# Block-diagonal keys of the second and third layer written by ScalarE instead of by copies through DMA

## The chip, the cores and the metric

One core of a Trainium2 chip runs the whole program. The metric is device time in microseconds (us); lower is better. The engines are TensorE (PE; PEld is its weight load), VectorE (DVE), ScalarE (ACT), GpSimd (POOL) and SyncE (SP, which here only issues transfers). SPq is SP's queue of transfers.

## The reference

Four transformer blocks run one after another on x of 32 x 128 x 256, with a context of the same shape. The change touches the second and the third block, which have the same form:

```
Q, K, V = split into 16 heads of 16 (x @ wq + bq, kv @ wk + bk, kv @ wv + bv)
A       = softmax(Q K^T / 4, masked)
x       = layernorm(x + (A V) @ wo + bo)          # self attention: kv = x
x       = the same once more with kv = context     # cross attention
x       = layernorm(x + relu(x @ w1 + b1) @ w2 + b2)
```

All is computed in float32. A product is made of three fp32r products of a high and a low part (L97).

## The kernel before

`phase16_full` computes the second layer and then, as a program section of its own, the third. The first layer is two sections before them, and the fourth layer (`Track`, tags "fourth") comes behind. A round is two of the 32 batch rows, 256 tokens, so a layer has 16 rounds (`ROUNDS2`). Tensors of the second layer have names with `second_`, those of the third `third_`.

The order on each engine is written out by hand in one `body(r)` per engine, and the engines meet through semaphores (`wait_ge`). One body has four steps, here called x0, x1, y0 and y1. In each step TensorE first makes the scores of the attention half that comes next (`pe_scores`, mask matmuls L1576 and score matmuls L1584), then turns the probabilities of the present half (`pe_turn`, L1595, four per step) and mixes those with V (`pe_mix`, L1608 and L1614). Between these it does projections, feed-forward products and the transposes of the norms (`Norm16.pe`, L1729) of other rounds, up to four rounds apart. ScalarE takes the exponentials (`act_exp`, L1641; four groups of four per step, t = 0 to 3), VectorE the maxima (L1621) and the copies of the turned probabilities (L1627).

The keys are made in step x1 for the self attention of the next round and in step y1 for the cross attention of this one. TensorE's `pe_k` leaves them in the shared PSUM bank `EV_BANK`; the next user of the bank waits until it is read. ScalarE's `act_k` (L1377) adds the bias and writes `a_k`. It stands between the exponentials t = 0 and t = 1 of the step. Behind t = 1 come `act_spread` (L1532) and the norm's `act` and `act_hi` (L1738 and L1746).

Two neighbouring heads have their scores made by one matmul with 32 rows, so a key operand `k_block` is needed with a second copy of the 256 tokens, in which the rows of the other head are zero. `pool_setup` sets `k_block` to zero once, and SP then copies the 16 rows of each head to their place (`sp_k`, L1402: 8 heads in each of 2 column groups, 16 copies of 16 x 256). `k_block` lies in `stage`, the buffer through which the weights come in at a layer's start. `pe_scores` waits for the copies. SP issues the copies in the same queue as the loads of the next inputs.

What of this runs at a layer's start, before the first body, is written at the end of each engine's function: the weights' split, K, Q and V of round 0, and the first scores.

## Time and profile before

| | us |
|---|---|
| median of 3 runs | 3672.21 (3661.26 to 3674.09) |
| the profiled execution, its own time | 3672.43 |
| its span in the trace | 3670.7 |
| TensorE busy | 3180.7 (87%) |
| VectorE busy | 2038.8 (56%) |
| ScalarE busy | 1938.2 (53%) |
| GpSimd busy | 1642.5 (45%) |

The busy times are sums over the whole program. The second layer lies at about 1520 to 2415 us of the span, the third at about 2415 to 3300 us.

### The profile page before, as it was taken

The numbers are of one execution on the slowest core, as the hardware profiler recorded it, in microseconds if no ns is written. First come the engines' busy times: TensorE is split into PE (matmuls) and PEld (weight loads), VectorE is DVE, ScalarE is ACT, GpSimd is POOL, SyncE is SP. The second block draws the span as 40 slices with busy tenths as digits, with TensorE's granted clock in tenths as the row PEclk, the third lists the DMA queues.
The fourth block names the chain that finished last, engine by engine and source line by source line (L and its number), as shares of the span: only waits on it lengthen the run. The fifth ranks groups of instructions, "written<-read, shape, count | busy, mean of one in ns | idle before, by whom it ended". The sixth has DMA issues, their size and how long they took to land. (4 is left out here: it accounts for less than half of the span.)

```text
span 3670.7 us, 79460 instructions
## 1 busy us (share of the span) xinstructions
PE 3180.7 (87%) x27248; PEld 2716.9 (74%) x27248; DVE 2038.8 (56%) x4126; ACT 1938.2 (53%) x7862; POOL 1642.5 (45%) x2020
## 2 busy tenths in 40 slices
PE   8999996899999998379999999737999999956987
PEld 5998895688888887357888888626888888754664
DVE  3455553444444444346777777525677777734665
ACT  2444442333333333156777777425777777635775
POOL 1223222024444435324666666622566666662444
PEclk9999998999999999779999999957999999988999
DMA  3112112101111110311221221021111111113231
GB/s 114 50 46 66 60 37 105 60 27 35 49 49 49 49 46 18 119 40 46 60 62 58 62 62 53 25 103 38 42 55 57 57 57 57 42 33 106 85 98 55
DMA packets 192554, 213.61 MB, mean 58 GB/s; under 512 B 30209, under 2 KB 161537, under 8 KB 189697
## 3 DMA queue, kind: packets, MB, share of 16 engines
q1 hardware_dynamic: 192384, 211.40, 18.1%
q8 instruction: 101, 1.65, 0.2%
q14 instruction: 69, 0.56, 0.1%
HBM read 131.59 MB, written 58.72 MB: 52 GB/s over the span
## 5 line engine op out<-in xcount | busy, mean ns | idle before, releaser
L1641 ACT ACTIVATE second_stage<-second_psum,second_neg_max 128x128 f32<-128x128 f32 x1024 | 362.7, 386 | 206.7 <-DVE second_neg_max L1621 206.4
L1641 ACT ACTIVATE third_stage<-third_psum,third_neg_max 128x128 f32<-128x128 f32 x1024 | 362.6, 386 | 193.4 <-DVE third_neg_max L1621 193.1
L1641 ACT ACTIVATION_READ_ACCUMULATOR second_stage<-second_psum,second_neg_max 128x1 f32 x1024 | 231.5, 226 | 0.0
L1641 ACT ACTIVATION_READ_ACCUMULATOR third_stage<-third_psum,third_neg_max 128x1 f32 x1024 | 231.1, 226 | 0.0
L534 POOL TENSOR_TENSOR cross_ff_hidden_lo<-cross_ff_relu,cross_ff_hidden_hi 128x256 fp32r<-128x256 f32 x128 | 93.3, 730 | 288.5 <-DVE cross_ff_hidden_hi L529 288.5
L1621 DVE TENSOR_REDUCE second_neg_max<-second_psum 128x4 f32<-128x512 f32 x256 | 169.2, 684 | 53.8 <-PE second_psum L1584 51.4
L1621 DVE TENSOR_REDUCE third_neg_max<-third_psum 128x4 f32<-128x512 f32 x256 | 168.7, 682 | 41.1 <-PE third_psum L1584 40.1
L1524 ACT ACTIVATE fourth_stage<-fourth_psum,fourth_neg_max 128x128 f32<-128x128 f32 x512 | 181.7, 386 | 3.8 <-DVE fourth_neg_max L1500 3.8
L1595 PE MATMUL third_psum<-third_eye,third_stage 128*128 128x128 f32 x1024 | 165.0, 285 | 16.8 <-DVE third_p_turned_odd L1627 7.9
L1595 PE MATMUL second_psum<-second_eye,second_stage 128*128 128x128 f32 x1024 | 162.8, 283 | 14.4 <-DVE second_p_turned_odd L1627 7.4
L529 DVE CAST cross_ff_hidden_hi<-cross_ff_relu 128x256 fp32r<-128x256 f32 x128 | 45.4, 355 | 209.7 <-ACT cross_ff_relu L524 209.6
L1595 PEld LDWEIGHTS third_psum<-third_eye,third_stage 128*128 128x128 f32 x1024 | 118.5, 144 | 46.4 <-issue 25.1
L1595 PEld LDWEIGHTS second_psum<-second_eye,second_stage 128*128 128x128 f32 x1024 | 118.2, 143 | 40.8 <-issue 21.2
L415 ACT ACTIVATE cross_arena<-cross_psum,cross_neg_max 128x128 f32<-128x128 f32 x256 | 90.4, 365 | 95.6 <-DVE cross_neg_max L448 95.6
L415 ACT ACTIVATE self_arena<-self_psum,self_neg_max 128x128 f32<-128x128 f32 x256 | 90.5, 366 | 84.6 <-DVE self_neg_max L448 84.6
L464 DVE TENSOR_TENSOR self_attended_lo<-self_psum,self_attended_hi 128x512 fp32r<-128x512 f32 x64 | 44.3, 692 | 159.4 <-ACT self_attended_hi L428 159.4
L1545 POOL COPY third_inverse_row<-third_inverse 128x128 f32<-128x128 f32 x128 | 33.9, 294 | 211.7 <-DVE third_inverse L1512 176.3
L524 ACT ACTIVATE cross_ff_relu<-cross_psum,cross_cols 128x256 f32<-128x256 f32 x128 | 60.7, 474 | 124.5 <-PE cross_psum L97 122.7
L1707 POOL TENSOR_SCALAR second_n_z<-second_n_z,second_n_moments,second_n_rstd 128x256 f32<-128x256 f32 x96 | 117.1, 1225 | 10.3 <-POOL second_n_rstd L1702 10.3
L1707 POOL TENSOR_SCALAR third_n_z<-third_n_z,third_n_moments,third_n_rstd 128x256 f32<-128x256 f32 x96 | 117.0, 1225 | 10.2 <-POOL third_n_rstd L1702 10.2
L1545 POOL COPY second_inverse_row<-second_inverse 128x128 f32<-128x128 f32 x128 | 34.0, 294 | 189.7 <-DVE second_inverse L1512 189.7
L1506 DVE COPY fourth_stage<-fourth_psum 128x512 f32<-128x512 f32 x128 | 87.7, 685 | 51.1 <-PE fourth_psum L1459 51.1
(438 smaller groups left out, 12548.7 us busy)
## 6 DMA issues: line engine op xcount, KB each, us to landing
second_stage<-second_a_k SPq DMA_DIRECT2D x512, 16.0 KB, 1.8
third_stage<-third_a_k SPq DMA_DIRECT2D x512, 16.0 KB, 1.8
cross_arena<-in_l0b_packed SPq DMA_DIRECT2D x6, 1024.0 KB, 4.9
self_arena<-in_l0a_packed SPq DMA_DIRECT2D x4, 1024.0 KB, 6.2
self_x_raw<-in_x_t SPq DMA_DIRECT2D x8, 512.0 KB, 3.8
self_x_rows<-in_x_rows SPq DMA_DIRECT2D x8, 512.0 KB, 3.9
self_ct_raw<-in_ctx_t SPq DMA_DIRECT2D x8, 512.0 KB, 4.3
context_hi<-self_ct_hi SPq DMA_DIRECT2D x8, 512.0 KB, 5.0
```

The source lines that it names most:

```text
L415: ins = act.activation(sh.p[:, h % 2, b, :], psum[:, S8_BANK, b * SEQ:(b + 1) * SEQ], ACT.Exp, bias=sh.neg_max[:, h % 2, b:b + 1], accum_o ...
L464: dve.tensor_tensor(self.sh.attended.lo[:, h % 2, :], psum[:, MIX8_BANK, :], f32(self.sh.attended.hi[:, h % 2, :]), ALU.subtract) \
L524: act.activation(self.relu[:, t % HIDDEN_SLOTS, :], psum[:, bank, 0:HALF], ACT.Relu, bias=self.b1[:, t % M:t % M + 1]).then_inc(self.hidde ...
L529: dve.tensor_copy(self.hidden.hi[:, t % HIDDEN_SLOTS, :], self.relu[:, t % HIDDEN_SLOTS, :]) \
L534: pool.tensor_tensor(self.hidden.lo[:, t % HIDDEN_SLOTS, :], self.relu[:, t % HIDDEN_SLOTS, :], f32(self.hidden.hi[:, t % HIDDEN_SLOTS, :] ...
L1506: dve.tensor_copy(self.sh.p_turned[:, h % 4, :, :], psum[:, TURN_BANK, :].rearrange("p (x k) -> p x k", x=4)) \
L1524: ins = act.activation(self.sh.p[:, h % 4, x, :], psum[:, SCORE_BANKS[h % 4], x * SEQ:(x + 1) * SEQ], ACT.Exp, bias=self.sh.neg_max[:, h % ...
L1545: ins = pool.tensor_copy(self.sh.inverse_row[:, b, k * P:(k + 1) * P].rearrange("p (g d) -> p g d", g=8), self.sh.inverse[:, b, k * 8:(k + ...
L1595: ins = pe.transpose(banks.psum[:, TURN_BANK, x * SEQ:(x + 1) * SEQ], self.sh.p_wide[:, 4 * b + t, x, :], self.sh.eye[:])
L1621: dve.tensor_reduce(self.sh.neg_max[:, 4 * b + t, :], psum[:, SCORE_BANKS[t], :].rearrange("p (x k) -> p x k", x=4), AX_X, ALU.max, negate ...
L1641: ins = act.activation(self.sh.p_wide[:, 4 * b + t, x, :], psum[:, SCORE_BANKS[t], x * SEQ:(x + 1) * SEQ], ACT.Exp, bias=self.sh.neg_max[: ...
L1707: pool.tensor_scalar(self.z[:, b, :], self.z[:, b, :], self.moments[:, b, 0:1], self.rstd[:, b:b + 1], ALU.subtract, ALU.mult) \
```

## The change

ScalarE writes both halves of `k_block` itself. `act_k` is four activations instead of two: for each column group c and each parity e it writes 256 columns, with a scale that is one [128,1] column of `parity` (1 in the rows of the heads with that parity, 0 in the others) and a bias that is multiplied with the same column, so that the other heads' rows come out as zero. The buffer `a_k`, the 16 copies per call and the zeroing by GpSimd are gone. `act_k` now waits for the scores of the round before, and `pe_scores` for `k_ready` instead of the copies. VectorE makes `parity` and the biases once per layer at its start. The fourth layer keeps the copies.

```diff
@@ -1316,11 +1316,11 @@
 class Project16:
 
 
-    def __init__(self, kit, name, w):
+    def __init__(self, kit, name, w, keys=True):
         sb = kit.sb
         self.w = w
         self.q = sb(name + "_q", [P, C, T2], F32)
-        self.k = sb(name + "_k", [P, C, T2], F32)
+        self.k = sb(name + "_k", [P, C, T2], F32) if keys else None
         self.v = sb(name + "_v", [P, B2, C, 4, 2, 32], F32)
         self.v_slots = [self.v[:, b].rearrange("p c j e f -> p (c j) (e f)").rearrange(
             "p g (x d) -> p g x d", d=DK)[:, :, 0:4:3, :] for b in range(B2)]
@@ -1329,7 +1329,8 @@
         self.q_ready = kit.counter(name + "_q_ready", 1)
         self.k_in_psum = kit.counter(name + "_k_in_psum", 1)
         self.k_ready = kit.counter(name + "_k_ready", C)
-        self.k_blocked = [kit.counter(f"{name}_k_blocked{c}", 16 * 8) for c in range(C)]
+        if keys:
+            self.k_blocked = [kit.counter(f"{name}_k_blocked{c}", 16 * 8) for c in range(C)]
         self.v_in_psum = kit.counter(name + "_v_in_psum", 1)
         self.v_ready = kit.counter(name + "_v_ready", 1)
 
@@ -1555,6 +1556,26 @@
                            ALU.subtract).then_inc(self.lo_ready.sem, 1)
 
 
+class ProjectWide(Project16):
+
+
+
+    def __init__(self, kit, name, w, k_block, sh):
+        Project16.__init__(self, kit, name, w, keys=False)
+        self.k_block, self.sh = k_block, sh
+
+    def act_k(self, act, r, psum, scores_read):
+
+        act.wait_ge(scores_read.sem, scores_read.at(r, 0))
+        act.wait_ge(self.k_in_psum.sem, self.k_in_psum.at(r, 1))
+        for c in range(C):
+            for e in range(2):
+                ins = act.activation(self.k_block[:, c, e, :], psum[:, EV_BANK, c * T2:(c + 1) * T2],
+                                     ACT.Identity, bias=self.w["k_bias_of"][:, e, c:c + 1],
+                                     scale=self.sh.parity[:, e:e + 1])
+            ins.then_inc(self.k_ready.sem, 1)
+
+
 class AttendWide(Attend16):
 
 
@@ -1564,8 +1585,7 @@
     def pe_scores(self, pe, r, banks, b):
         if b == 0:
             pe.wait_ge(self.proj.q_ready.sem, self.proj.q_ready.at(r, 1))
-            for c in range(C):
-                pe.wait_ge(self.proj.k_blocked[c].sem, self.proj.k_blocked[c].at(r, 16 * 8))
+            pe.wait_ge(self.proj.k_ready.sem, self.proj.k_ready.at(r, C))
             if self.mask is not None:
                 pe.wait_ge(self.mask.ready.sem, self.mask.ready.at(r, 1))
         tokens = slice(b * SEQ, (b + 1) * SEQ)
@@ -1873,6 +1893,9 @@
         self.spread = sb("spread", [P, B2, DM], F32)
         self.mix = sb("mix", [P, B2, DM], F32)
         self.attended = Split(kit, "attended", [P, C, T2])
+        if wide:
+            self.in_head = sb("in_head", [P, 8], F32)
+            self.parity = sb("parity", [P, 2], F32)
         self.minus_half = sb("minus_half", [P, 4], F32)
         self.eye = sb("eye", [P, P], F32)
 
@@ -1904,6 +1927,8 @@
             self.ct = Split(kit, "ct", [P, C, T2])
             self.x_rows = kit.sb("x_rows", [P, B2, DM], F32)
             self.residual = kit.sb("residual", [P, B2, DM], F32)
+            self.k_bias_of = [kit.sb(f"k_bias{i}", [P, 2, C], F32) for i in range(2)]
+            self.parity_made = kit.counter("parity_made", 0)
         self.small_loaded = kit.counter("small_loaded", 0)
         self.hi_made = kit.counter("w_hi_made", 0)
         self.lo_made = kit.counter("w_lo_made", 0)
@@ -1943,7 +1968,7 @@
         n = str(i + 1)
         return {"q": self.take(i * 2048, 512, DM), "k": self.take(i * 2048 + 512, 512, DM),
                 "v": self.take(i * 2048 + 1024, 512, DM), "q_bias": self.colv("q" + n),
-                "k_bias": self.colv("k" + n), "v_row": self.rowv("v" + n)}
+                "k_bias": self.colv("k" + n), "k_bias_of": self.k_bias_of[i] if self.extra else None, "v_row": self.rowv("v" + n)}
 
     def out_of(self, i):
         return self.take(i * 2048 + 1536, 512, DM)
@@ -1993,7 +2018,7 @@
                 if not m.per_batch:
                     m.pool(pool, 0)
         pool.wait_ge(consts.sem, made)
-        for s in range(2):
+        for s in range(0 if self.extra else 2):
             pool.wait_ge(self.lo_made.sem, min(s + 1, self.slots))
             pool.memset(sh.stage[:, s * sh.block_cols:(s + 1) * sh.block_cols], 0.0) \
                 .then_inc(self.block_zeroed.sem, 1)
@@ -2026,8 +2051,7 @@
         kit, sh, psum, mask = layer.kit, layer.sh, layer.psum, layer.mask
         xt, ct, rowv, colv = layer.xt, layer.ct, layer.rowv, layer.colv
         stored = kit.counter("stored", 32)
-        proj1, proj2 = (Project16(kit, f"a{i + 1}", layer.weights_of(i)) for i in range(2))
-        proj1.k_block, proj2.k_block = sh.k_block
+        proj1, proj2 = (ProjectWide(kit, f"a{i + 1}", layer.weights_of(i), sh.k_block[i], sh) for i in range(2))
         att1, att2 = (AttendWide(kit, f"a{i + 1}", (proj1, proj2)[i], mask[i], layer.out_of(i), sh)
                       for i in range(2))
         y1_rows = kit.sb("y1_rows", [P, B2, DM], F32)
@@ -2106,16 +2130,12 @@
                     store(Back(r, 4), r, 4)
                 if ok(0) and not (isinstance(r, int) and r == 0):
                     load_context(r, r, 0)
-                if ok(1):
-                    proj1.sp_k(sp, Back(r, -1))
                 if ok(2):
                     load_mask(mask[0], Back(r, -2), r, -2)
                 if ok(1):
                     load_rows(Back(r, -1), r, -1)
                 if ok(2):
                     load_x(Back(r, -2), r, -2)
-                if ok(0):
-                    proj2.sp_k(sp, r)
                 if ok(1):
                     load_mask(mask[1], Back(r, -1), r, -1)
 
@@ -2126,8 +2146,6 @@
             load_mask(mask[0], 0, 0, 0)
             load_mask(mask[1], 0, 0, 0)
             load_x(1, 1, 0)
-            sp.wait_ge(layer.block_zeroed.sem, 2)
-            proj1.sp_k(sp, 0)
             load_mask(mask[0], 1, 1, 0)
             for r in range(FULL_FIRST):
                 body(r)
@@ -2171,7 +2189,7 @@
 
                 exp(x1_next, 0)
                 if ok(1):
-                    proj1.act_k(act, Back(r, -1), psum)
+                    proj1.act_k(act, Back(r, -1), psum, att1.scores_ready)
                 exp(x1_next, 1)
                 spread(x1)
                 if ok(-2):
@@ -2194,7 +2212,7 @@
 
                 exp(y1_next, 0)
                 if ok(0):
-                    proj2.act_k(act, r, psum)
+                    proj2.act_k(act, r, psum, att2.scores_ready)
                 exp(y1_next, 1)
                 spread(y1)
                 if ok(0):
@@ -2206,7 +2224,8 @@
                 exp(y1_next, 3)
 
             act.wait_ge(layer.lo_made.sem, layer.slots)
-            proj1.act_k(act, 0, psum)
+            act.wait_ge(layer.parity_made.sem, 3)
+            proj1.act_k(act, 0, psum, att1.scores_ready)
             proj1.act_q(act, 0, psum)
             for t in range(4):
                 att1.act_exp(act, 0, psum, 0, t)
@@ -2223,11 +2242,23 @@
             for proj in (proj1, proj2):
                 dve.memset(proj.v[:], 0.0).then_inc(layer.zeroed.sem, 1)
             layer.dve_split_weights(dve, 0)
+            dve.wait_ge(layer.consts.sem, 2)
+            dve.tensor_reduce(sh.in_head[:], sh.eye[:].rearrange("p (h d) -> p h d", d=DK), AX_X, ALU.max) \
+               .then_inc(layer.parity_made.sem, 1)
+            dve.wait_ge(layer.parity_made.sem, 1)
+            dve.tensor_reduce(sh.parity[:], sh.in_head[:].rearrange("p (a e) -> p e a", e=2), AX_X, ALU.max) \
+               .then_inc(layer.parity_made.sem, 1)
+            dve.wait_ge(layer.parity_made.sem, 2)
             dve.wait_ge(layer.small_loaded.sem, 16 * 3)
             for i in range(2):
                 dve.tensor_scalar(colv(f"q{i + 1}"), colv(f"q{i + 1}"), DK ** -0.5, None, ALU.mult)
             dve.tensor_tensor(rowv("s1"), rowv("s1"), rowv("o2"), ALU.add)
             dve.tensor_tensor(rowv("s2"), rowv("s2"), rowv("ff"), ALU.add)
+            for i in range(2):
+                for e in range(2):
+                    ins = dve.tensor_scalar(layer.k_bias_of[i][:, e, :], colv(f"k{i + 1}"),
+                                            sh.parity[:, e:e + 1], None, ALU.mult)
+            ins.then_inc(layer.parity_made.sem, 1)
             for norm in (norm1, norm2, norm3):
                 ins = dve.memset(norm.stats[:], 0.0)
             ins.then_inc(layer.biases.sem, 1)
```

Three places in the order of the instructions. First, SP's queue at the start of the second layer; before:

```order
L2079 DMA second_ct_lo<-context_lo 128x2x256
L2085 DMA second_x_rows<-x_rows 128x2x256
L1836 DMA second_mask_ints<-in_mask_self 128x2x128
L1836 DMA second_mask_ints<-in_mask_cross 128x2x128
L2072 DMA second_xt_hi<-x_hi 128x2x256
L2072 DMA second_xt_lo<-x_lo 128x2x256
L1402 DMA second_stage<-second_a_k 16x256 x16
L1836 DMA second_mask_ints<-in_mask_self 128x2x128
L1402 DMA second_stage<-second_a_k 16x256 x16
L1836 DMA second_mask_ints<-in_mask_self 128x2x128
L2085 DMA second_x_rows<-x_rows 128x2x256
```

The same place in the changed kernel:

```order
L2103 DMA second_ct_lo<-context_lo 128x2x256
L2109 DMA second_x_rows<-x_rows 128x2x256
L1856 DMA second_mask_ints<-in_mask_self 128x2x128
L1856 DMA second_mask_ints<-in_mask_cross 128x2x128
L2096 DMA second_xt_hi<-x_hi 128x2x256
L2096 DMA second_xt_lo<-x_lo 128x2x256
L1856 DMA second_mask_ints<-in_mask_self 128x2x128 x2
L2109 DMA second_x_rows<-x_rows 128x2x256
```

The sixteen copies of round 0, and those of every later round, are gone; the loads behind them move up and keep their order.

Second, ScalarE in step x1 of the loop of the second layer, from the exponentials t = 0 to t = 2; before:

```order
L1641 ACTIVATE second_stage,second_sums<-second_psum,second_neg_max 128x128 x4
L1374 REGISTER_ALU
L1375 REGISTER_ALU
L1377 ACTIVATE second_a_k<-second_psum,second_cols 128x256 x2
L1638 REGISTER_ALU
L1641 ACTIVATE second_stage,second_sums<-second_psum,second_neg_max 128x128 x4
L1532 COPY second_spread<-second_psum 128x256
L1738 ACTIVATE second_n_y<-second_psum,second_cols 128x256 x2
L1746 CAST second_n_yt_hi<-second_n_y 128x512
L1638 REGISTER_ALU
L1641 ACTIVATE second_stage,second_sums<-second_psum,second_neg_max 128x128 x4
```

The same place in the changed kernel:

```order
L1661 ACTIVATE second_stage,second_sums<-second_psum,second_neg_max 128x128 x4
L1569 REGISTER_ALU
L1570 REGISTER_ALU
L1573 ACTIVATE second_stage<-second_psum,second_k_bias,second_parity 128x256 x4
L1658 REGISTER_ALU
L1661 ACTIVATE second_stage,second_sums<-second_psum,second_neg_max 128x128 x4
L1533 COPY second_spread<-second_psum 128x256
L1758 ACTIVATE second_n_y<-second_psum,second_cols 128x256 x2
L1766 CAST second_n_yt_hi<-second_n_y 128x512
L1658 REGISTER_ALU
L1661 ACTIVATE second_stage,second_sums<-second_psum,second_neg_max 128x128 x4
```

The two activations that wrote `a_k` are four that write `k_block` in `stage`, ahead of the same instructions.

Third, VectorE at the start of the second layer in the changed kernel:

```order
L2002 TENSOR_TENSOR second_w_lo<-second_stage,second_w_hi 128x2048
L2246 TENSOR_REDUCE second_in_head<-second_eye 128x8
L2249 TENSOR_REDUCE second_parity<-second_in_head 128x2
L2254 TENSOR_SCALAR second_cols<-second_cols 128x2 x2
L2255 TENSOR_TENSOR second_rows<-second_rows,second_rows_extra 128x256
L2256 TENSOR_TENSOR second_rows<-second_rows,second_rows_extra 128x256
L2259 TENSOR_SCALAR second_k_bias<-second_cols,second_parity 128x2 x4
L2263 MEMSET second_n_stats 128x12 x3
L2002 TENSOR_TENSOR second_w_lo<-second_stage,second_w_hi 128x2048 x3
```

L2246, L2249 and L2259 are new, six small instructions between the splits of the first and of the second part of the weights.

## Rows read from the trace of the kernel before

**Rows 1.** The page's slices: busy tenths of TensorE and its clock, 40 slices.

```profile
PE   8999996899999998379999999737999999956987
PEclk9999998999999999779999999957999999988999
```

**Rows 2.** Windows: busy us of PE, PEld, DVE, ACT, POOL; clock, DMA share, GB/s.

```profile
1560.00:1580.00 20.00, 11.40 (x52) 5.45 (x52) 6.60 (x11) 9.42 (x53) 0.53 (x2) 0.50 0.04 10
1900.00:2000.00 100.00, 97.43 (x1029) 83.14 (x1019) 72.56 (x155) 73.20 (x331) 66.45 (x87) 1.00 0.21 62
2900.00:3000.00 100.00, 95.64 (x1026) 82.27 (x1026) 73.39 (x160) 73.27 (x333) 63.27 (x84) 1.00 0.21 63
```

**Rows 3.** TensorE's waits, second layer: us in total, times, longest us.

```profile
PE second_psum L1576 <- DMA second_stage<-second_a_k: 12.9, 1, 12.9
PE second_psum L97 <- DVE second_n_yt_lo L1752: 7.4, 13, 1.3
PEld second_psum L97 <- ACT second_n_y L1738: 3.7, 15, 1.3
```

**Rows 4.** Timeline, starts of both layers: start, us, what, [idle before <- releaser].

```profile
1541.48 2.17 POOL L1849 TENSOR_SCALAR second_mask_flags<-second_mask_ints 128x256 bf16<-128x256 int32 x1 [2.48 <-issue]
1543.00 0.84 ACT L1377 ACTIVATE second_a_k<-second_psum,second_cols 128x256 f32<-128x256 f32 x2 [2.41 <-DVE second_w_lo L1977]
1550.79 10.08 SPq L1402 DMA_DIRECT2D second_stage<-second_a_k  x16
1562.31 1.87 PE L1576 MATMUL second_psum<-second_mask_flags,second_mask_eye 128*128 128x512 bf16 x4 [12.87 <-DMA second_stage<-second_a_k]
2462.77 1.87 PE L1576 MATMUL third_psum<-third_mask_flags,third_mask_eye 128*128 128x512 bf16 x4 [12.84 <-DMA third_stage<-third_a_k]
```

**Rows 5.** Two ScalarE lines: duration ns min/median/max.

```profile
L1377 ACT ACTIVATE second_a_k<-second_psum,second_cols x64: 466/488/498, 1543.0 to 2316.1; 128x256 f32<-128x256 f32 x64
L1738 ACT ACTIVATE second_n_y<-second_psum,second_cols x96: 553/564/625, 1605.8 to 2411.2; 128x256 f32<-128x256 f32 x96
```

**Rows 6.** Timeline, second layer, one step x1.

```profile
1959.76 0.85 ACT L1377 ACTIVATE second_a_k<-second_psum,second_cols 128x256 f32<-128x256 f32 x2
1960.47 0.39 ACT L1641 ACTIVATE second_stage<-second_psum,second_neg_max 128x128 f32<-128x128 f32 x1
1961.58 0.63 PE L1729 MATMUL second_psum<-second_eye,second_n_z 128*128 128x128 f32 x4 [0.16 <-POOL second_n_z L1707]
1961.84 0.43 ACT L1532 COPY second_spread<-second_psum 128x256 f32<-128x256 f32 x1
1962.32 1.02 ACT L1738 ACTIVATE second_n_y<-second_psum,second_cols 128x256 f32<-128x256 f32 x2
1963.37 0.63 ACT L1746 CAST second_n_yt_hi<-second_n_y 128x512 fp32r<-128x512 f32 x1
1964.03 1.63 DVE L1752 TENSOR_TENSOR second_n_yt_lo<-second_n_y,second_n_yt_hi 128x512 fp32r<-128x512 f32 x1 [0.38 <-ACT second_n_yt_hi L1746]
1965.71 0.38 PE L97 MATMUL second_psum<-second_n_yt_hi,second_w_lo 128*128 128x256 f32 x1 [0.51 <-DVE second_n_yt_lo L1752]
```

**Rows 7.** Timeline, second layer, one step y1.

```profile
1934.62 0.37 ACT L1641 ACTIVATE second_stage<-second_psum,second_neg_max 128x128 f32<-128x128 f32 x1 [4.27 <-DVE second_neg_max L1621]
1936.00 0.85 ACT L1377 ACTIVATE second_a_k<-second_psum,second_cols 128x256 f32<-128x256 f32 x2
1938.52 1.02 ACT L1738 ACTIVATE second_n_y<-second_psum,second_cols 128x256 f32<-128x256 f32 x2
1939.59 0.19 PEld L97 LDWEIGHTS second_psum<-second_n_yt_hi,second_w_lo 128*128 128x128 f32 x1 [0.17 <-ACT second_n_y L1738]
```

**Rows 8.** Timeline, third layer, one step x1.

```profile
3000.47 1.02 ACT L1738 ACTIVATE third_n_y<-third_psum,third_cols 128x256 f32<-128x256 f32 x2 [0.27 <-PE third_psum L1729]
3003.66 0.39 PE L97 MATMUL third_psum<-third_n_yt_hi,third_w_lo 128*128 128x256 f32 x1 [0.32 <-DVE third_n_yt_lo L1752]
```

**Rows 9.** Timeline, second layer, step x1 of round 1.

```profile
1629.86 0.66 PE L1595 MATMUL second_psum<-second_eye,second_stage 128*128 128x128 f32 x4 [1.85 <-DVE second_p_turned_odd L1627]
```

## The prediction

> **What bounds the kernel now.** I read the slices of the page first, then windows of the two layers, the waits, and last the timeline of single steps. TensorE is the busy engine nearly everywhere [rows 1], and in the middle of the second and the third layer it is busy 96 to 97 us in 100 at full clock, while ScalarE is at 73 [rows 2]. So in the steady part only what makes TensorE wait costs time, and almost nothing does. The copies of the keys appear in its waits exactly once in the second layer, with 12.9 us [rows 3]: that is the layer's start. In every later round the copies are issued and landed a step or two before the scores that need them. They are 16 instructions in 10.08 us of SP's queue [rows 4], and hidden.
>
> What TensorE does wait for in the steady part is short and comes often: 13 times the low part of a norm's output (7.4 us in all), which VectorE makes in step x1, and 15 times ScalarE's L1738 ahead of a weight load (3.7 us), in step y1 [rows 3]. Both come from one chain on ScalarE: exponentials, keys, exponentials t = 1, spread, norm, cast. The keys stand in the middle of it, in both steps. This matters more than ScalarE's busy share.
>
> **The start of a layer: a gain.** Before, ScalarE writes round 0's keys at 1543.00 [rows 4], TensorE does Q and V, and then stands 12.87 us until the sixteen copies have landed; in the third layer 12.84 us [rows 4]. After the change nothing is copied. The first scores then need Q and K, which are both read before V is computed, and the mask flags, which GpSimd has finished at 1541.48 + 2.17 = 1543.65 [rows 4]. So they can follow V at once. The longer `act_k` gives back a part, since Q's product waits for the bank that it reads. Its new length comes from rows 5 and 6. An activation with one column operand (the bias) takes 488 ns, and a pair takes 0.85 us, the next instruction starting 0.71 us after the pair's start, or 0.355 us for each. L1738 has the same shape with two column operands, bias and scale, as the new ones have: 564 ns [rows 5], and a pair takes 1.02 us [rows 6], so the second starts 1.02 - 0.56 = 0.46 us behind the first. Four of these hold the engine for 4 x 0.456 = 1.82 us and end after 3 x 0.456 + 0.564 = 1.93 us. The bank is free 1.93 - 0.85 = 1.08 us later. Gain: 12.87 - 1.08 = 11.8 us and 12.84 - 1.08 = 11.8 us, together 23.5.
>
> The Trainium skill (ScalarE: Activation LUTs, What ACT_TABLE_LOAD costs) puts 93 ns on each column operand and says that activations back to back overlap by 93 ns; the rows have 76 ns for the operand and about 0.11 to 0.13 us for the overlap. By the page's figures, 280 ns + 0.833 ns per column with one operand, four activations instead of two would add 4 x 0.49 - 2 x 0.40 = 1.17 us where the rows give 1.11; over the calls below that is an estimate of 66 us instead of 63. I take the rows.
>
> VectorE's six new small instructions lie between the first split of the weights and the second, where ScalarE and VectorE wait for the weights' transfers. I cost them at nothing. Without that cover they are about 1 us a layer, by my estimate. GpSimd's zeroing went beside other work and gives nothing.
>
> A second part of the start is the clock. After the long wait the first 20 us of the fill ran at a granted 0.50, the lower level, with TensorE busy 11.40 us [rows 2]. If the wait is gone, a part of that work may run at the upper level. Between nothing and half of the busy time (5.7 us) lies the gain; much of the fill is ScalarE's and VectorE's chain, so I take 2 us a layer, 4 in all.
>
> **Every later call: a loss.** ScalarE goes on after `act_k` 1.82 - 0.71 = 1.11 us later. What stands behind it?
>
> Step x1, second layer [rows 6]. The exponentials t = 1 start at 1960.47 as soon as the keys are issued, spread at 1961.84, L1738 at 1962.32, the cast at 1963.37, VectorE's low part at 1964.03, and TensorE's L97 at 1965.71, having waited 0.51 us. ScalarE has no gap in this chain, and TensorE waits at its end already. So the whole 1.11 us arrives at TensorE. A second way leads there too: the transposes L1729 need the bank that the keys free. The keys ended at 1960.61 and now end at 1961.69, and TensorE started L1729 at 1961.58. That is hardly 0.2 us, and it lies inside the 1.11.
>
> Step y1, second layer [rows 7]. The keys are at 1936.00, L1738 ends at 1939.54, and TensorE's weight load for the next feed-forward product starts at 1939.59, having waited 0.17 us for just that. Again there is no slack: another 1.11 us.
>
> Then ScalarE stands idle 4.27 us at the start of the next key step, until the maxima come [rows 7], which follow TensorE's scores. The delay is therefore not carried on; ScalarE, VectorE and TensorE are all later by the same amount, and the next step has its old relations. For the same reason nothing gives the time back: TensorE's other short waits are for chains that moved with it.
>
> Third layer, x1 [rows 8]: L1738 had waited 0.27 us for TensorE's transposes, so 1.11 - 0.27 = 0.84 us pass on; TensorE's L97 waited 0.32 us at the end. Its y1 I take like the second layer's.
>
> Calls: 32 a layer, one of them at the start, 15 in x1 and 16 in y1. In x1 the call of round 0 falls into the fill with idle ScalarE, and I cost it at nothing. Round 1 has no norm there, but the turned probabilities hang on spread, for which TensorE waited 1.85 us [rows 9], so it pays in full. That leaves 14 + 16 = 30. Second layer: 30 x 1.11 = 33.3. Third: 13 x 0.84 + 17 x 1.11 = 29.8. Together 63.1 us.
>
> The scores' own wait for the copies and SP's earlier loads are worth nothing in the steady part; no load appears among the waits that I list [rows 3].
>
> **The sum.** 63.1 - 23.5 - 4 = +35.6 us. The profiled execution took 3672.4, as the median of the runs did (3672.2), so 3672.4 + 35.6 = 3708.0.
>
> **The rivals.**
> Half absorbed: only one of the two key steps passes its delay on. For it speaks that the waits at the chain's end are short (0.17 and 0.32 us), so that an unseen reserve of queued TensorE work might cover them; against it, that there is a wait at all. 31.5 - 27.5 = +4: 3676.
> Faster: the two chains take the longer `act_k` without TensorE feeling it, for instance because the four activations overlap more tightly than L1738's, and only the start counts: -27.5, 3645. The point from which the change is a gain is 23.5 / 60 = 0.39 us per call, where the rows say 1.11 for the engine; even a scale column that costs nothing leaves two more at 0.355 us, 0.71 us per call. So this needs slack that no row shows.
> No start gain: something else holds the first scores or the fill swallows the 23.5 us, and the full loss stays: +63, 3735. The mask flags are ready, but TensorE's first products in the fill hang on chains that may have other ends.
> That the change doesn't do what it says I exclude: the copies are gone from the queue.
>
> **How the numbers follow.** Full loss with start gain 0.66 (by itself 3692 to 3722, which takes the clock at its two ends and some tenths per call), half absorbed 0.15, faster 0.07, no start gain 0.12. A measurement of this kernel tells about 0.5%, 18 us, from no change. Slower: 0.66 + 0.12, less 0.02 for the lower edge, 0.76. Same: 0.15 + 0.02, 0.17. Faster 0.07. The range 3678 to 3730 leaves out the faster case (0.07), half of the half absorbed one (0.07) and a part of the last (0.05).
>
> **What would show it.** In the profile after: no DMA at the first scores, and the scores of each layer about 11.8 us earlier against the layer's start. Four key activations near 564 ns each, 1.8 us from the first to the next exponential. In x1 TensorE's wait for the low part near 1.6 us instead of 0.5 (1.2 in the third layer), in y1 a wait of about 1.2 us for L1738; a round 2.2 us longer in the second layer, 1.95 in the third. The prediction is wrong if the rounds keep their length, if the start doesn't shrink, or if the clock falls in the steady part.

## The result, and the profile after

The changed kernel takes 3706.8 us, the median of 4 runs (3703.7 to 3709.9); the kernel before, on the same chip, 3669.6 (3661.3 to 3674.1). The ratio is 1.010, with a 95% interval of 1.008 to 1.013: the change costs about 1%. The profiled execution took 3704.3 us, with a span of 3702.6, which is 31.9 more than the span before.

The page of the changed kernel: totals of the engines, and TensorE's row and clock row in the 40 slices.

```profile
PE 3176.7 (86%) x27123; PEld 2715.3 (73%) x27248; DVE 2049.2 (55%) x4138; ACT 2007.1 (54%) x7990; POOL 1641.2 (44%) x2016
...
PE   8999996889999997479999999747999999866887
...
PEclk9999998999999998689999999968999999988998
```

The slices can hardly be told from those of before [rows 1]; a loss of 1 us in every 24 doesn't show there. The windows do show it (columns as in [rows 2]: length, busy us of PE, PEld, DVE, ACT, POOL, clock, DMA share, GB/s).

```profile
1560.00:1580.00 20.00, 15.46 (x133) 12.05 (x126) 8.80 (x15) 8.96 (x39) 3.31 (x5) 0.64 0.06 18
1900.00:2000.00 100.00, 93.82 (x972) 79.15 (x965) 69.69 (x149) 73.54 (x322) 62.80 (x83) 1.00 0.15 47
2900.00:3000.00 100.00, 92.55 (x966) 79.58 (x966) 69.45 (x149) 75.70 (x333) 59.65 (x78) 1.00 0.13 42
```

In the middle of the two layers TensorE is busy 93 to 94 us in 100 where it was 96 to 97, at the same full clock. ScalarE's share is hardly higher, though each round gives it about 2.2 us more to do, because the round has become as much longer. The clock stays at its upper level in these stretches, so it has no part in the loss. In the first row, the fill, TensorE does more in the same 20 us than before, and the granted clock is 0.64 instead of 0.50; but the fill now begins 14 us earlier (rows below), so the row is a later part of it. Over the same stage, from the first scores to the key activations of y1 in round 0, the granted clock is 0.72 instead of 0.69, and in the third layer 0.77 instead of 0.68.

The starts of both layers, timeline (start, us, what, [idle before <- releaser]):

```profile
1538.37 2.05 POOL L1869 TENSOR_SCALAR second_mask_flags<-second_mask_ints 128x256 bf16<-128x256 int32 x1 [20.41 <-DMA second_mask_ints<-in_mask_self]
1539.78 1.93 ACT L1573 ACTIVATE second_stage<-second_psum,second_k_bias,second_parity 128x256 f32<-128x256 f32 x4 [2.41 <-DVE second_w_lo L2002]
...
1548.36 1.93 PE L1596 MATMUL second_psum<-second_mask_flags,second_mask_eye 128*128 128x512 bf16 x4
...
2467.97 1.31 PE L1596 MATMUL third_psum<-third_mask_flags,third_mask_eye 128*128 128x512 bf16 x4
```

The scores start 1548.36 - 1539.78 = 8.58 us behind the first key activation, where it was 1562.31 - 1543.00 = 19.31 [rows 4]: a gain of 10.7 us. The third layer has 8.58 as well, and gains 11.9. The four activations take 1.93 us, and TensorE has no wait for a DMA left.

One step x1 in the middle of the second layer, timeline, the step that answers to [rows 6]:

```profile
1961.58 1.95 ACT L1573 ACTIVATE second_stage<-second_psum,second_k_bias,second_parity 128x256 f32<-128x256 f32 x4
1963.38 0.41 ACT L1661 ACTIVATE second_stage<-second_psum,second_neg_max 128x128 f32<-128x128 f32 x1
1963.58 0.66 PE L1749 MATMUL second_psum<-second_eye,second_n_z 128*128 128x128 f32 x4 [0.34 <-ACT second_stage L1573]
...
1965.00 1.11 ACT L1758 ACTIVATE second_n_y<-second_psum,second_cols 128x256 f32<-128x256 f32 x2
...
1966.63 0.66 PE L1615 MATMUL second_psum<-second_eye,second_stage 128*128 128x128 f32 x4 [0.53 <-DVE second_p_turned_odd L1647]
1966.80 1.78 DVE L1772 TENSOR_TENSOR second_n_yt_lo<-second_n_y,second_n_yt_hi 128x512 fp32r<-128x512 f32 x1 [0.22 <-ACT second_n_yt_hi L1766]
1968.63 0.39 PE L97 MATMUL second_psum<-second_n_yt_hi,second_w_lo 128*128 128x256 f32 x1 [0.63 <-DVE second_n_yt_lo L1772]
```

From the first key activation to the next exponential it is 1963.38 - 1961.58 = 1.80 us, as forecast; before, 0.71 [rows 6]. TensorE now waits three times in this step, 0.34 us for the keys themselves at L1749, 0.53 us for the turned probabilities, and 0.63 us for the low part. Before, it waited 0.16 us at the same transposes, for GpSimd's `n_z`, and 0.51 us for the low part.

The step y1 that answers to [rows 7]:

```profile
1986.88 1.95 ACT L1573 ACTIVATE second_stage<-second_psum,second_k_bias,second_parity 128x256 f32<-128x256 f32 x4
1988.88 0.66 PE L1749 MATMUL second_psum<-second_eye,second_n_z 128*128 128x128 f32 x4 [0.35 <-ACT second_stage L1573]
...
1991.47 0.39 PE L97 MATMUL second_psum<-second_n_yt_hi,second_w_lo 128*128 128x256 f32 x1 [0.78 <-ACT second_n_y L1758]
```

TensorE's waits over the whole second layer, 1520 to 2420 us (us in total, times, longest):

```profile
PE second_psum L1615 <- DVE second_p_turned_odd L1647: 16.8, 18, 3.0
PE second_psum L97 <- ACT second_n_y L1758: 13.3, 16, 1.1
PE second_psum L1749 <- POOL second_n_z L1727: 12.4, 5, 6.0
PE second_psum L1749 <- ACT second_stage L1573: 11.8, 27, 2.6
...
PE second_psum L97 <- DVE second_n_yt_lo L1772: 8.9, 13, 1.3
```

The same view before:

```profile
PE second_psum L1729 <- POOL second_n_z L1707: 24.2, 32, 7.4
...
PE second_psum L1595 <- DVE second_p_turned_odd L1627: 7.4, 6, 1.8
...
PE second_psum L97 <- ACT second_n_y L1738: 3.3, 3, 1.1
```

The 12.9 us for the copies [rows 3] are gone. The wait for the keys' writes at the transposes, 27 times, is new by name only: before, the same transposes waited as often for GpSimd's `n_z`, and both kernels wait 24.2 us there in all (12.4 + 11.8 after). What has grown is the wait for the turned probabilities, from 7.4 to 16.8 us, and that for L1758, from 3.3 to 13.3 us.

How the 31.9 us come about can be summed from the starts of the layers' first key activations, as all work is laid out between them. The first layer, which is unchanged, gave -3.2 (1543.00 to 1539.78; such a scatter is between any two executions). From the second layer's first keys to the third's it is 919.6 us instead of 899.3, **+20.3**; from the third's to the fourth's 896.3 instead of 879.8, **+16.5**; the rest, from the fourth layer's first keys on, gave -1.7. The forecast had 33.3 - 11.8 - 2 = 19.5 and 29.8 - 11.8 - 2 = 16.0 for the two.

### The profile page after: what moved, and what is told of

The parts are those of the page before. It is cut to its first block and busy times, and to the rows that moved or that the text cites. A ratio compares the mean times of both kernels' runs of the same rounds, so it can differ in the third digit from the quotient of the medians.

```text
span 3702.6 us, 78263 instructions
## 1 busy us (share of the span) xinstructions
PE 3176.7 (86%) x27123; PEld 2715.3 (73%) x27248; DVE 2049.2 (55%) x4138; ACT 2007.1 (54%) x7990; POOL 1641.2 (44%) x2016
## 5 line engine op out<-in xcount | busy, mean ns | idle before, releaser
L1615 PE MATMUL second_psum<-second_eye,second_stage 128*128 128x128 f32 x1024 | 163.6, 284 | 23.8 <-DVE second_p_turned_odd L1647 16.8
L97 PE MATMUL third_psum<-third_n_yt_hi,third_w_lo 128*128 128x256 f32 x320 | 98.6, 308 | 23.4 <-ACT third_n_y L1758 13.4
L97 PE MATMUL second_psum<-second_n_yt_hi,second_w_lo 128*128 128x256 f32 x320 | 98.7, 308 | 23.2 <-ACT second_n_y L1758 13.3
```

The costliest lines, as they stand in the source:

```text
L97: ins = pe.matmul(out, w, x, start=first and n == 0, stop=last and n == total - 1, skip_group_check=skip)
L1615: ins = pe.transpose(banks.psum[:, TURN_BANK, x * SEQ:(x + 1) * SEQ], self.sh.p_wide[:, 4 * b + t, x, :], self.sh.eye[:])
```

## The experiments

Two theories stood against each other. **The chain:** a key call delays ScalarE in the middle of a chain without slack, and each us of it arrives at TensorE, whoever reads what. **The bank:** the loss comes from EV_BANK being released later, for which TensorE's transposes and products wait (the row with 27 waits for L1573 would be its sign). A third one, the plain share of busy time, says that any added work on ScalarE costs the same wherever it stands. "Round" below is the distance of the q calls of successive rounds, in us, in the middle of each layer. All ratios are to the kernel before on the same chip: its median there is 3674.3 for e1 to e4, 3671.1 for e5 to e8 and 3671.7 for e9 to e12.

```
kernel                       median us  ratio [95%]             round, 2nd / 3rd layer
before                        3669.6                            47.91 / 46.84
after                         3706.8    1.010 [1.008, 1.013]    50.10 / 49.02
e1_two_writes                 3643.5    0.993 [0.991, 0.994]    47.97 / 46.89
e2_copies_and_four            3737.7    1.018 [1.017, 1.020]    50.09 / 48.99
e3_extra_behind_release       3737.4    1.018 [1.016, 1.020]    50.20 / 49.06
e4_six_writes                 3771.3    1.026 [1.024, 1.028]    51.93 / 50.83
e5_no_scale_column            3685.2    1.004 [1.002, 1.006]    49.33 / 48.23
e6_first_round_only           3645.9    0.993 [0.991, 0.996]    47.98 / 46.87
e7_split_with_vector          3660.2    0.997 [0.996, 0.999]    48.56 / 47.48
e8_norm_ahead                 3721.9    1.015 [1.013, 1.017]    50.16 / 49.64
e9_norm_ahead_copies          3738.1    1.018 [1.016, 1.020]    49.70 / 49.59
e10_extra_in_idle             3670.9    1.000 [0.999, 1.001]    48.00 / 46.93
e11_keys_in_idle              3646.0    0.992 [0.990, 0.994]    48.10 / 46.92
e12_extra_behind_exps         3675.3    1.000 [0.999, 1.002]    48.11 / 47.12
```

**e1: the start alone.** The changed kernel with two activations a call, without scale column, into one half of the buffer; the other half stays zero, so a part of the scores is left out.

```
         for c in range(C):
+            act.activation(self.k_block[:, c, 0, :], psum[:, EV_BANK, c * T2:(c + 1) * T2],
+                           ACT.Identity, bias=self.w["k_bias"][:, c:c + 1]).then_inc(self.k_ready.sem, 1)
```

> The changed kernel, but ScalarE writes only the first half of each column group of the key operand, with the bias column and no scale column: two activations per call as before the change, no copies (the other half stays as zeroed, so part of the scores is left out). The engine time of a call is that of before, so only the layers' starts should differ from it. My theory (the longer chain on ScalarE costs, the start gains): 12 us per layer less than before, about -24 to -28 us, 3643 to 3646. Rival 'the start's gain is swallowed by the fill': within 5 us of before, 3670. Rival 'something else in the change costs, not the number of activations' (the new waits, the writes into the stage buffer, VectorE's set-up): well above 3670.

Measured: 0.993, and the rounds keep the length of before. The start's gain is real and stands alone; the rounds' loss needs the longer `act_k`.

**e2: the calls' length alone.** The kernel before with its copies, and each key call as long as after: one more activation for each c into a spare tile, each with a second column operand.

```
+        scale = 1.0 if self.ones is None else self.ones[:, 0:1]
         for c in range(C):
...  (where there is a spare tile)
+            act.activation(self.spare[:, c, :], psum[:, EV_BANK, c * T2:(c + 1) * T2],
+                           ACT.Identity, bias=self.w["k_bias"][:, c:c + 1], scale=scale)
```

> The kernel before with all its copies, but each key call in the second and third layer has four activations with two column operands: the two real ones and one each into a spare buffer, all before the bank is given back. My theory: 60 calls that pay 1.05 to 1.11 us, and at the start the longer call once per layer: +65 us, about 3735, more than the changed kernel by the start's gain. Rival 'the loss comes from what replaced the copies': near 3670.

Measured: 3737.7, the rounds as in the changed kernel to 0.03 us. So the copies by DMA were worth nothing in the steady part. Against the kernel before on its own chip e2 loses 63.4 us and the changed kernel 37.2, and the 26 us between them are what the copies' removal gave at the start.

**e3: the bank's release.** As e2, but the two additional activations stand behind the release and read weights in SBUF, so the bank is held only by the two real ones.

```
+            for c in range(C):
+                act.activation(self.spare[:, c, :], f32(self.w["q"].hi[:, c, :]), ACT.Identity,
+                               bias=self.w["k_bias"][:, c:c + 1], scale=scale)
```

> As the run with copies and four activations, but the two into the spare buffer read a weight tile in SBUF instead of the bank and come behind the two real ones, so the bank is given back after two activations. It separates the engine time from the time that the bank is held. My theory (engine time ahead of spread and the norm): still +1.0 us for about 60 calls, +55 to +65 us, 3725 to 3735. Rival 'the bank': what costs is that TensorE's transposes get the bank 1.08 us later; then only the scale column's 0.2 us per call is left, about +10 us, 3680.

Measured: 3737.4, the rounds 50.20 and 49.06. With the bank free early the loss is the same. TensorE's transposes wait for GpSimd again as in the kernel before (1600 to 2360 us):

```profile
PE second_psum L1735 <- POOL second_n_z L1713: 6.9, 29, 1.4
```

The bank theory is refuted for four activations on ScalarE: the waits for L1573 are time that TensorE would otherwise spend waiting elsewhere in the same step.

**e4: one more pair.** The changed kernel with a third activation for each c.

```
+            ins = act.activation(self.spare[:, c, :], psum[:, EV_BANK, c * T2:(c + 1) * T2],
+                           ACT.Identity, bias=self.w["k_bias_of"][:, 0, c:c + 1],
+                           scale=self.sh.parity[:, 0:1])
```

> The changed kernel with six activations per call instead of four: one more per column group, into a spare buffer, before the bank is given back. A dose. My theory: no slack anywhere, 0.91 us more for each of some 60 calls and the start 0.9 later: +56 us over the changed kernel, about 3763, +93 over before. Rival 'a part of the four activations is still hidden': the step is larger per activation than from two to four (63 us for two), up to 0.91 x 62 + what was hidden; rival 'other engines take over': smaller, under 40 us.

Measured: 1.83 and 1.81 us a round over the changed kernel, for two calls, 0.91 us each, which is 2 x 0.456 us. The loss is linear in ScalarE's time.

**e5: the scale column.** The changed kernel, four activations with the bias alone; both halves then hold all rows.

```
                 ins = act.activation(self.k_block[:, c, e, :], psum[:, EV_BANK, c * T2:(c + 1) * T2],
-                                     ACT.Identity, bias=self.w["k_bias_of"][:, e, c:c + 1],
-                                     scale=self.sh.parity[:, e:e + 1])
+                                     ACT.Identity, bias=self.w["k_bias_of"][:, e, c:c + 1])
```

> The changed kernel with four activations per call, but without the scale column (both halves get all rows, so the scores are not the reference's). It sizes the operand. The engine time of a call is then 4 x 0.355 = 1.42 us, 0.71 over before instead of 1.11. My theory: 60 x 0.71 = 43, less 24 to 28 for the start and the clock, +15 to +19 over before, about 3688, that is 20 us or more under the changed kernel. Rival 'the number of instructions or of bank reads counts, not their length': as the changed kernel, 3708.

The lines of the key activations in e1, e2, e5 and the changed kernel, one from each (duration ns min/median/max):

```profile
L1572 ACT ACTIVATE second_stage<-second_psum,second_cols x64: 466/487/497, 1544.1 to 2303.1; 128x256 f32<-128x256 f32 x64
```

```profile
L1380 ACT ACTIVATE second_spare<-second_psum,second_cols,second_ones x64: 560/578/593, 1538.1 to 2346.1; 128x256 f32<-128x256 f32 x64
```

```profile
L1573 ACT ACTIVATE second_stage<-second_psum,second_k_bias x128: 466/494/512, 1540.2 to 2321.2; 128x256 f32<-128x256 f32 x128
```

```profile
L1573 ACT ACTIVATE second_stage<-second_psum,second_k_bias,second_parity x128: 557/586/601, 1539.8 to 2334.5; 128x256 f32<-128x256 f32 x128
```

The second column costs 586 - 494 = 92 ns of an instruction. Measured, a round of e5 is 1.42 us longer than before, 0.71 us a call: two activations more at 0.355 us, exactly as the prediction's bound for a column that costs nothing. The column is the other 0.38 us of a call's 1.09.

**e6: direct writes in the first round only.** The changed start and, in all later rounds, the old `act_k` with its copies.

```
+        if not first_round(r):
...
+            for c in range(C):
+                act.activation(self.k[:, c, :], psum[:, EV_BANK, c * T2:(c + 1) * T2], ACT.Identity,
+                               bias=self.w["k_bias"][:, c:c + 1]).then_inc(self.k_ready.sem, 1)
+            return
```

> ScalarE writes both halves itself only in round 0 of each layer; from round 1 on two activations write a_k and SP copies as before. If start and steady part are separate, as my theory has it, this keeps the whole gain and pays once per layer in y1 of round 0: -22 to -27 us against before, about 3646. Rival 'the loss is not in the calls' (set-up, waits): less gain. Rival 'the copies of round 1 now come too late in the short fill': TensorE waits for the copies in the first rounds and up to 10 us per layer are lost again.

Measured: 3645.9 us, 0.993 [0.991, 0.996], the rounds as before. Only the gain is left: this version beats both kernels.

**e7: half of the writes on VectorE.** The changed kernel; ScalarE writes c = 0, VectorE c = 1.

```
-        for c in range(C):
+        for c in range(C - 1):
...
+            ins = dve.tensor_scalar(self.k_block[:, c, e, :], psum[:, EV_BANK, c * T2:(c + 1) * T2],
+                                    self.sh.parity[:, e:e + 1], self.w["k_bias_of"][:, e, c:c + 1],
+                                    ALU.mult, ALU.add)
```

> The changed kernel with the second column group's two writes on VectorE, between its second copy of turned probabilities and its fourth maximum, where VectorE waited about 0.9 us for spread later on; it reads the bank after ScalarE's two. ScalarE's call takes 0.91 us, 0.20 over before. My theory: 60 x 0.2 = 12 less 24 to 28 for the start: -12 to -16 us, about 3657. Rival 'VectorE has no room either, or the bank comes back too late': VectorE's writes end as late as ScalarE's four did, TensorE's transposes wait as long as after the change, and the result is at or above 3670.

Measured: 3660.2, a round 0.65 us longer than before, 0.33 a call where 0.20 was worked out. Here the bank seems to matter. TensorE's wait, 1600 to 2360 us:

```profile
PE second_psum L1759 <- DVE second_stage L1583: 14.1, 27, 0.7
```

The transposes wait 27 times, 0.52 us each, for VectorE to have read the bank. My reading is that, with ScalarE's chain relieved, the bank is the next thing that is late; it is read from the waits, and no run tries it.

**e8 and e9: the order on ScalarE.** If only the chain to the norm's output counts, the norm should go ahead of the exponentials t = 1, which would take the delay instead. e8 does that in the changed kernel, e9 in the kernel before.

```
-                exp(x1_next, 1)
...  (spread, norm.act and act_hi stay as they are)
+                exp(x1_next, 1)
```

The same in step y1.

> The changed kernel with another order on ScalarE in x1 and y1: spread, the norm's activations and its cast stand ahead of the exponentials t = 1, directly behind the keys. All work is the same. My theory (it is the chain keys, t = 1, spread, norm, cast that TensorE waits for, and ScalarE has 4 us to spare per step): the norm no longer stands behind 1.4 us of exponentials, its start is given by TensorE's transposes, and most of the 63 us are gone: -15 to -35 us against before, about 3648. Rival 'the engine time itself is what counts' (ScalarE as a bound): no change against the changed kernel, 3708. Rival 'the bank': the transposes wait for the keys to end, some 0.2 to 0.5 us per call stay, 3660 to 3675.

> The kernel before with the order of the run with the norm ahead: spread, norm and cast before the exponentials t = 1 in x1 and y1. The run with the norm ahead fell out slower, with new waits for the exponentials and the ReLU that now stand last in the step. If in a key step every output of ScalarE is due without slack, so that any order only picks which one is late, this costs here too: +20 to +40 us over before, 3690 to 3710. If the new waits came only from the longer keys, it is within 10 us of before.

Both came out the other way: e8 is at 1.015, slower than the changed kernel, and e9, which adds no work at all to the kernel before, at 1.018. (The mean of e9's third layer holds one longer round; the others there are 49.40.) A step of e9 on ScalarE, timeline, then ScalarE's waits from 1600 to 2350 us:

```profile
1975.12 0.37 ACT L1532 COPY second_spread<-second_psum 128x256 f32<-128x256 f32 x1 [0.84 <-PE second_psum L1614]
1976.00 1.02 ACT L1738 ACTIVATE second_n_y<-second_psum,second_cols 128x256 f32<-128x256 f32 x2 [0.51 <-PE second_psum L1729]
```

```profile
ACT second_spread L1532 <- PE second_psum L1614: 27.2, 31, 1.6
ACT second_n_y L1738 <- PE second_psum L1729: 16.1, 30, 1.6
```

And TensorE's waits in the same stretch:

```profile
PE second_psum L1576 <- ACT second_stage L1641: 19.9, 24, 3.0
PE second_psum L1729 <- ACT second_ff_relu L1803: 17.0, 12, 1.4
```

ScalarE now stands idle in the middle of the step, 0.84 us for TensorE's mix and 0.51 us for its transposes: time that the exponentials t = 1 had filled. Everything behind is later, the last exponentials and the ReLU too, and TensorE waits for those: for the ReLU up to 1.4 us, for the exponentials up to 3.0. That is where my picture was too narrow. Not one chain has no slack, but nearly all that ScalarE does between the maxima's arrival and the end of the key step, and the order of before fills its waits.

**e10 and e12: the same work where ScalarE is free.** The kernel before with two more activations a call, as in e3, in other places: in e10 behind the last exponentials of x0 and y0, that is in the idle time before the next maxima; in e12 behind the last exponentials of x1 and y1, the key steps themselves.

```
+        def extra(act):
+            for c in range(C):
+                act.activation(spare[:, c, :], f32(proj1.w["q"].hi[:, c, :]), ACT.Identity,
+                               bias=proj1.w["k_bias"][:, c:c + 1], scale=ones[:, 0:1])
...
+                    extra(act)
```

> The kernel before with its copies, and two extra activations (two column operands, from SBUF into a spare buffer, about 1.0 us together, the same as in the run with the extra behind the release) twice per round, but behind the last exponentials of the steps x0 and y0, where ScalarE then waits about 4 us for the maxima. Same instructions, same total of ScalarE as there, where they cost 63 us. My theory (the place decides): 0 to +8 us over before. Rival 'ScalarE's total per round counts': +50 us or more.

> As the run with the extra in the idle time, but behind the last exponentials of the key steps x1 and y1, so behind everything on my chain. Theory 'only the chain to the norm counts': 0 to +10 us. Theory 'each thing ScalarE does in a key step and just behind it is due': ReLU and norm of the next step come 1 us later where they had 0 to 0.6 us of room: +20 to +50 us.

The extra activations in e10 and the idle time that is left behind them, timeline:

```profile
1954.37 1.14 ACT L2036 ACTIVATE second_spare<-second_w_hi,second_cols,second_ones 128x256 f32<-128x256 f32 x2
...
1958.76 0.37 ACT L1641 ACTIVATE second_stage<-second_psum,second_neg_max 128x128 f32<-128x128 f32 x1 [3.25 <-DVE second_neg_max L1621]
```

Measured: ratios of 1.000 for both. The kernel e3 issues the same two activations as often, but right behind the keys, and costs 1.8%. (About 0.2 of its 1.1 us a call is the second column of the two real activations, 2 x 92 ns, which e10 and e12 don't have.) So ScalarE's busy share is refuted as an explanation, and the place decides. e12 says more exactly where the line runs: behind a key step's last exponential the time is free to within 0.1 us a call in the second layer and 0.14 in the third.

**e11: the keys by ScalarE, but in the idle time.** No copies by DMA: `act_k` writes `a_k` as before, and behind the last exponentials of the next step, x0 or y0, two activations spread it into `k_block`. Self attention's first call writes directly.

```
+            ins = act.activation(self.k_block[:, :, e, :], self.k[:], ACT.Copy,
+                                 scale=self.sh.parity[:, e:e + 1])
...
+                if ok(-1):
+                    proj2.act_spread_keys(act, Back(r, 1), att2.scores_ready)
```

> No copies by DMA, but the keys are read from the bank by two activations as before, and two activations of 128 x 512 with the scale column put them into the two halves at the end of the next step (y0 and x0), in ScalarE's idle time; round 0's self attention keys are written directly as in the change. About 1.25 us per call, moved out of the key steps. My theory: the start's gain without the loss, as the run that keeps the copies from round 1 on: -22 to -27 us, 3646. Rival 'the end of x0 and y0 has less than 1.25 us of room before the next scores': +0.2 us or more per call, 3655 to 3670.

The new instructions, and e11's windows in the middle of both layers:

```profile
L1582 ACT ACTIVATE second_stage<-second_a_k,second_parity x62: 712/772/839, 1579.7 to 2319.5; 128x512 f32<-128x512 f32 x62
```

```profile
1900.00:2000.00 100.00, 97.35 (x1003) 83.12 (x999) 72.15 (x153) 78.33 (x337) 66.05 (x86) 1.00 0.15 49
2900.00:3000.00 100.00, 96.64 (x1005) 82.96 (x1003) 71.11 (x156) 80.59 (x346) 61.16 (x82) 1.00 0.13 42
```

Measured: 3646.0 us, 0.992 [0.990, 0.994]. ScalarE is busier (78 and 81 in 100) than in the changed kernel (74 and 76), and TensorE is back at 97. What the change sets out to do, zeros by a scale column and no copies, gains 0.8% if it stands where ScalarE has time, and loses 1% where the diff put it. Its place isn't quite free: a round of the second layer is 0.19 us longer than before. e6 and e11 beat both kernels and can't be told from each other.

## Why the prediction was right

**Bound and sign.** Right. TensorE's short waits for ScalarE's chain were the thing to look at, at 73% busy ScalarE; e10 against e3 shows it. The prediction said +35.6 us on its profiled execution; the spans differ by 31.9, and the medians by 37.2. That the sum came so close is in part luck, as the third layer shows below.

**The start, 11.8 us a layer.** 10.7 and 11.9. The copies' wait went and nothing took its place. The second layer got 1.1 less than 11.8 because V's product now ran at a granted clock of 0.50 instead of 1.00, with 0.21 us from matmul to matmul against 0.12; in the third layer it had the lower level in both kernels. e1, e6 and e11 confirm the size: they are 25 to 31 us under before, and 27.5 were summed with the clock.

**The clock, 2 us a layer.** From the first scores to the key activations of y1 in round 0 the fill took 39.85 us instead of 41.45, and in the third layer 38.82 instead of 41.37: 1.6 and 2.55. That all of it comes from the clock (0.72 for 0.69 and 0.77 for 0.68) isn't shown.

**1.11 us a call.** 1.09: the rounds grew by 2.19 us in the second layer, and the exponentials follow the first key activation after 1.80 us instead of 0.71. The activations are 586 ns each in the profile, not near 564, but they still follow one another every 0.45 us. e4 and e5 show each part of it, 0.91 us for a pair with two columns and 0.71 for one without. VectorE's six small instructions and GpSimd's zeroing aren't priced by a run of their own; in both kernels the first keys wait for the same split of the weights, for 2.41 us.

**0.84 us a call in x1 of the third layer.** This term of the sum was mis-sized. The third layer's rounds grew by 2.18 us, not 1.95, so x1 paid about 1.1. I had followed the chain through L1738 alone and set off its 0.27 us of waiting. The step before, and the same step after, timeline:

```profile
3001.77 1.28 POOL L2006 TENSOR_TENSOR third_residual<-third_x_rows,third_rows 128x512 f32<-128x512 f32 x1
3002.18 1.43 DVE L1752 TENSOR_TENSOR third_n_yt_lo<-third_n_y,third_n_yt_hi 128x512 fp32r<-128x512 f32 x1 [0.59 <-ACT third_n_yt_hi L1746]
```

```profile
3023.92 1.11 ACT L1758 ACTIVATE third_n_y<-third_psum,third_cols 128x256 f32<-128x256 f32 x2
...
3025.66 1.29 POOL L2031 TENSOR_TENSOR third_residual<-third_x_rows,third_rows 128x512 f32<-128x512 f32 x1
3025.71 1.78 DVE L1772 TENSOR_TENSOR third_n_yt_lo<-third_n_y,third_n_yt_hi 128x512 fp32r<-128x512 f32 x1 [0.22 <-ACT third_n_yt_hi L1766]
3027.55 0.39 PE L97 MATMUL third_psum<-third_n_yt_hi,third_w_lo 128*128 128x256 f32 x1 [0.64 <-DVE third_n_yt_lo L1772]
```

GpSimd's residual runs beside VectorE's low part, and that ends 3027.49 - 3026.95 = 0.54 us behind the residual's end, however early it began. Before it was the same: residual 3001.77 + 1.28, low part 3002.18 + 1.43, 0.56 us apart. So it isn't L1738 but the residual that sets the end, and the residual follows spread, mix, cast and `attended_lo`, a way in which there is no 0.27 us to lose.

The second layer has the same, before and after:

```profile
1963.83 1.28 POOL L2006 TENSOR_TENSOR second_residual<-second_x_rows,second_rows 128x512 f32<-128x512 f32 x1
```

```profile
1966.75 1.28 POOL L2031 TENSOR_TENSOR second_residual<-second_x_rows,second_rows 128x512 f32<-128x512 f32 x1
```

The low part of [rows 6] ends 0.55 us behind the first, that of the step x1 above 0.55 us behind the second. Without the residual the low part of [rows 6], which takes 0.68 us where it runs alone, would have ended 0.95 us earlier. So there too the way through L1738 had slack, against the prediction's "no gap in this chain", and the 1.11 us came by the other way. The two ways part only behind spread, on which both hang: from spread's start to the low part's end it is 3.82 to 3.84 us in both layers, before and after. That the overlap is the cause was read from these rows and not tried by a run; the term is worth 13 x 0.27 = 3.5 us, and with it the third layer would have been forecast at +19.5, against the +16.5 measured.

Two things hid this error. Start and clock of this layer gave 0.7 us more than forecast. And the fourth to the sixth key call of the third layer, in rounds 1 and 2, cost 0.6 us together instead of 3.3: counted from the layer's first keys, the fourth call starts 13.4 us earlier than before and the seventh still 12.8, while behind it each call takes 1.1 back. (In e2 the same three calls cost 0.4 us.) Why they pay less isn't shown. So the +16.0 forecast and the +16.5 measured agree by luck. The total came out under the forecast because the unchanged parts gave -3.2 and -1.7, which is scatter.

**Where the waits show.** The forecast had the whole delay at the chain's end, 1.6 us for the low part in x1 and 1.2 for L1738 in y1. It is there in sum but not in one place: in x1 0.34 + 0.53 + 0.63 against 0.16 + 0.51, in y1 0.35 + 0.78 against 0.18 (for `n_z` at the transposes; the 0.17 of [rows 7] was a weight load's wait, and the matmuls behind it had none). TensorE meets the delayed engine at several points of a step, and what it waits at the first it doesn't wait at the last. The rows named add up to 0.83 and 0.95 us more than before, not to 1.1. All of TensorE's waits of a round grow from 1.3 to 3.1 us, shorter ones included; the other 0.4 us of the 2.2 are in its busy time, 47.18 us instead of 46.77 for the same 484 recorded matmuls. So the round's length is the measure, and not the waits.

**The reason behind it.** "Nothing gives the time back" held in the steady part, but the single chain was too narrow a reason, as e8 and e9 show: the exponentials and the ReLU ahead of the last exponential are due as well. The rivals fell: half absorbed by the rounds (2.19 and 2.18 us), no start gain by the start, faster by both.

## What to carry to other kernels

Price added work by where its engine stands idle, not by the engine's share of busy time: some 1 us of ScalarE a call cost 1.8% of the kernel between a step's maxima and its last exponential (e2, e3), and nothing that can be measured behind that (e10, e12). Look for the engine's long idle time in each step (here 4.2 us before the maxima), and move work that isn't due there, as e11 does; the copies by DMA that landed in time cost nothing here (a round is 47.98 us with them in e6 and 47.97 without them in e1), and only at a layer's start, where nothing hid them, were they worth replacing (e6). And before moving an instruction ahead of another, see which waits the other fills.

## What the runs showed of the hardware

- VectorE's low part, 128x512 from two tiles in SBUF, takes 0.68 us at its fastest and, in the steady rounds, 1.42 to 1.79 beside GpSimd's 128x512 residual, which began first and keeps its 1.28. It ends 0.55 us behind it each time. The Trainium skill (SBUF — State Buffer, Who interferes with whom) has a VectorE instruction with two inputs from SBUF contend with a GpSimd instruction that reads SBUF, for a port pair that it calls an exclusive lock; the trace agrees for the residual. Not every neighbour costs as much: beside GpSimd's mask flags (0.87 us, begun 0.14 us earlier) the low part takes 0.80 to 0.82.
- A second column operand adds 92 ns (494 to 586). The same instruction with its input from SBUF is slower than from PSUM, in e3 618 ns against e2's 578, and the next one starts 0.49 us behind it instead of 0.45:

```profile
L1383 ACT ACTIVATE second_spare<-second_w_hi,second_cols,second_ones x64: 591/618/624, 1546.0 to 2352.4; 128x256 f32<-128x256 f32 x64
```

- The profile's duration of an activation depends on how far it overlaps the instruction ahead of it. L1758, the same instruction as L1738 before, has a median of 647 ns where that had 564 [rows 5]. In the kernel before L1738 takes 564 ns where spread has ended and 616 where it starts 0.16 us before the end of an exponential; after the change L1758 starts 0.19 us before spread's end and takes 652. From one to the next of a pair it is 0.46 us in both kernels:

```profile
L1758 ACT ACTIVATE second_n_y<-second_psum,second_cols x96: 554/647/657, 1591.4 to 2428.3; 128x256 f32<-128x256 f32 x96
```
